# Stage B of a graph layer: rows that chunks 2 and 3 share with the next round's chunks 0 and 1 are summed there, and a load stands ahead of a wait

## What is computed

```python
h = relu(layernorm(x))
x = x + mean_over_edges(h[src] -> dst) @ W_l.T + h @ W_r.T      # layer 0, stage A
h = relu(layernorm(x))                                          # layer 1, stage B
agg = segment_sum(edge_attr, src, num_segments=N)
h = concatenate([h, agg], axis=1)
h = bn(silu(h @ W1 + b1))                                       # stage C, statistics over all nodes
h = bn(silu(h @ W2 + b2))                                       # stage F
x = x + h @ W3 + b3                                             # stage G
```

## Time and profile before

| | |
|---|---|
| median of three runs | 1505.77 us |
| the profiled execution, its own time | 1503.21 us |
| its span | 1501.3 us |
| POOL busy | 828.5 us, 55% |
| DVE busy | 1099.7 us, 73% |
| PE busy | 1021.5 us, 68% |
| ACT busy | 862.9 us, 57% |
| granted TensorE clock, mean | 0.918 |
| line 848, B's scatter | 196 instructions, 314.7 us busy, 168.5 us idle ahead of them |

### The profile page before, as it was taken

The page is one execution under the profiler, slowest core; times in us unless marked ns, Lnnn a source line. Parts: engine busy times, 40 slices in busy tenths (PEclk is TensorE's granted clock), DMA queues, the critical chain, the costliest instruction groups (busy, mean ns, idle before and its releaser), DMA issues.

```text
span 1501.3 us, 22959 instructions
## 1 busy us (share of the span) xinstructions
PE 1021.5 (68%) x5247; PEld 726.3 (48%) x5247; DVE 1099.7 (73%) x4644; ACT 862.9 (57%) x1686; POOL 828.5 (55%) x601
## 2 busy tenths in 40 slices
PE   0237767677666667658777777776657877997866
PEld 0125555555544455435444444444435765446755
DVE  1438888888867766669788878776764877778978
ACT  0226777777755555537666666656564545665533
POOL 6778887888888888766666667655551000000000
PEclk9959999999999988969999999889997998999989
DMA  9988898877766666677777777899987996207999
GB/s 277 386 275 220 204 228 211 187 166 169 170 146 142 135 144 143 140 159 199 196 195 197 193 195 198 234 264 273 268 247 250 348 333 234 97 28 260 407 403 373
DMA packets 225365, 333.72 MB, mean 222 GB/s; under 512 B 35778, under 2 KB 87242, under 8 KB 225300
## 3 DMA queue, kind: packets, MB, share of 16 engines
q1 hardware_dynamic: 157516, 285.22, 56.1%
q0 software_dynamic: 62720, 38.57, 20.4%
q10 hardware_dynamic: 5064, 9.29, 1.7%
HBM read 179.20 MB, written 153.80 MB: 222 GB/s over the span
## 4 chain that ended last, share of the span: by engine, by line
POOL 41%; DMA 26%; issue 16%; PE 10%; DVE 5%; SPq 1%; ACT 1%; POOLq 0%; DVEq 0%; ACTq 0%
POOL acc L833 20%; POOL acc L848 11%; DMA acc<-zT,target_b 8%; DMA acc<-tabs,target_b 8%; POOL xin L811 7%; PE ps L1538 6%; POOL zT L819 4%; DMA zT<-x_dram 3%; DMA xin<-acc 2%; PE ps L1548 1%; DMA acc<-zT,tabs 1%; DVE zT L1383 1%; DVE zT L1387 1%; PE ps L1514 1%; PE ps L1517 1%
## 5 line engine op out<-in xcount | busy, mean ns | idle before, releaser
L1430 PE MATMUL ps<-zT 128*128 128x512 f32 (+5 forms) x784 | 278.0, 505 | 196.4 <-ACT zT L951 135.4
L833 POOL DMA_INDIRECT acc<-zT,tabs x196 | 314.8, 1606 | 71.5 <-issue 64.6
L1430 PEld LDWEIGHTS ps<-zT 128*128 128x128 f32 (+1 forms) x784 | 162.6, 217 | 338.8 <-issue 208.8
L848 POOL DMA_INDIRECT acc<-zT,target_b x100 | 161.0, 1610 | 87.1 <-DMA acc<-zT,target_b 32.5
L1153 DVE SCALAR_TENSOR_TENSOR zT<-zT 128x128 f32<-128x128 f32 (+3 forms) x392 | 192.9, 548 | 12.7 <-DMA zT<-row_dram 6.4
L1221 DVE BATCH_NORM_STATS2 zT<-zT 128x6 f32<-128x128 f32 (+1 forms) x384 | 78.9, 278 | 165.3 <-DMA zT<-in_x_dram 165.3
L848 POOL DMA_INDIRECT acc<-tabs,target_b x96 | 153.7, 1601 | 81.4 <-issue 32.0
L811 POOL DMA_INDIRECT xin<-in_x_dram,tabs x140 | 141.9, 1014 | 47.3 <-issue 42.4
L1422 PE MATMUL ps<-ident,zT 128*128 128x128 f32 (+1 forms) x784 | 111.5, 288 | 65.4 <-ACT zT L904 65.4
L1422 PEld LDWEIGHTS ps<-ident,zT 128*128 128x128 f32 (+1 forms) x784 | 92.2, 149 | 78.4 <-ACT zT L904 75.7
L1548 PE MATMUL ps<-w,hT 128*128 128x128 f32 (+1 forms) x784 | 101.5, 285 | 38.2 <-DVE zT L1387 28.7
(11 more groups left out here) (159 smaller groups left out, 2017.0 us busy)
## 6 DMA issues: line engine op xcount, KB each, us to landing
acc<-bst SPq DMA_DIRECT2D x12, 2112.0 KB, 21.5
acc<-bst SPq DMA_DIRECT2D x48, 528.0 KB
zT<-row_dram SPq DMA_DIRECT2D x98, 256.0 KB, 5.7
zT<-in_x_dram SPq DMA_DIRECT2D x48, 512.0 KB, 6.7
zT<-acc SPq DMA_DIRECT2D x48, 512.0 KB, 4.3
zT<-x_dram SPq DMA_DIRECT2D x42, 512.0 KB, 8.5
out_dram<-zT SPq DMA_DIRECT2D x42, 512.0 KB, 7.7
zT<-in_edge_attr_dram SPq DMA_DIRECT2D x48, 256.0 KB, 6.4
```

The lines of the kernel that those rows point to most:

```text
L833: pool.indirect_dma_start(acc1, bass.IndirectOffsetOnAxis(ap=target_a[:, k, j:j + 1], axis=0), v[:, j, :], None, compute_op=ALU.add).then_ ...
L848: pool.indirect_dma_start(acc2, bass.IndirectOffsetOnAxis(ap=target_b[:, k, j:j + 1], axis=0), vrow_b[k % RING][:, j, :], None, compute_op ...
L1430: ins = nc.tensor.matmul(psA[:, 0:j + 1, 0:p], t[0:p, j, :], same[0:p, par, at:at + j + 1, 0:p], start=(j == ROWS - 1), stop=(j == 0))
```

## The change

In B, the rows of **chunks 2 and 3** that the next round names again are moved there. Chunk 3's are added into chunk 0 or chunk 1 of the next round, chunk 2's into its chunk 0. DVE gets one more comparison for each round (line 1188 of the new code, two chunks of names against chunk 3's), and `more`, `alone` and the corrected `count` are two columns wide. PE gets three products where it had one. POOL's chunk 0 then awaits chunks 0 and 1 of the round before, chunk 1 awaits chunk 2 (`s_mid2`), chunk 2 awaits chunk 3. The new matrices lie in `bst`, which also holds the zeros that clear `acc2`; so the first pair that is compared is rounds 1 and 2, round 1's chunk 0 awaits all of round 0, and DVE awaits the clearing ahead of B's rounds. SP's load of `acc1`'s rows stands ahead of the wait for chunk 3's landing, no longer behind it. Two pairs of semaphores of C and G become one pair, with the counts added.

```diff
@@ step_b, SP
                 i, par, tail, spill, slot = now
-                sp.wait_ge(*this(s_end2, par, i, 16))
                 if ahead:
                     load_b_nodes(*ahead)
+                sp.wait_ge(*this(s_end2, par, i, 16))
                 sp.wait_ge(*this(B["added"], par, i))
@@ scatter_b, POOL
                 if k:
-                    pool.wait_ge(*last(s_sc2, par, i, 48))
+                    pool.wait_ge(*last(s_sc2, par, i, 32))
+                if k == 1:
+                    pool.wait_ge(*last(s_mid2, par, i, 16))
+                    pool.wait_ge(*last(s_end2, par, i, 16))
                 for j in range(ROWS):
-                    if k and j == 1:
+                    if k > 1 and j == 1:
+                        pool.wait_ge(*last(s_mid2, par, i, 16))
+                    if k > 1 and j == 2:
                         pool.wait_ge(*last(s_end2, par, i, 16))
...
-                        .then_inc((s_end2 if j == ROWS - 1 else s_sc2)[par], 16)
+                        .then_inc((s_sc2, s_sc2, s_mid2, s_end2)[j][par], 16)
@@ compare_carry, DVE
+                nc.vector.scalar_tensor_tensor(
+                    carried_3[par][:, :, 0:p], irow[:, par, 0:2, 0:p], cols[:, before, 0, ROWS - 1:ROWS],
+                    alone[:, before, 1:2].unsqueeze(2).broadcast_to([P, 2, p]), ALU.is_equal, ALU.mult,
+                    accum_out=more[:, par, 1:2])
                 link_(nc.vector.scalar_tensor_tensor(
-                    carried[par][:, 0:p], irow[:, par, 0, 0:p], cols[:, before, 0, ROWS - 1:ROWS],
-                    alone[:, before:before + 1].broadcast_to([P, p]), ALU.is_equal, ALU.mult,
-                    accum_out=more[:, par:par + 1]))
+                    carried_2[par][:, 0:p], irow[:, par, 0, 0:p], cols[:, before, 0, ROWS - 2:ROWS - 1],
+                    alone[:, before, 0:1].broadcast_to([P, p]), ALU.is_equal, ALU.mult,
+                    accum_out=more[:, par, 0:1]))
@@ ahead of B's rounds, DVE
+            dve.wait_ge(s_zero2, 16 * RF)
@@ edge_product, PE
-                    given = carry is not None and j == 0
...
+                    taken_over = [] if carry is None or j > 1 else [(carried_3[par][:, j, :], ROWS - 1)]
+                    if taken_over and j == 0:
+                        taken_over.append((carried_2[par], ROWS - 2))
```

More of the change, by code:

```diff
@@ L203, in gnn_layers @@
         iota_c = part([P, COLS // 2]).bitcast(fp16)
-        carried = [iota_c[:, :].bitcast(fp32)[:, 0:P], tabs[:, 2 * GROUP:2 * GROUP + P]]
         cols = part([P, 2, 4, ROWS])
         count = sb("count", [P, 2, ROWS])
-        more = sb("more", [P, 2])
-        alone = sb("alone", [P, 2])
+        more = sb("more", [P, 2, 2])
+        alone = sb("alone", [P, 2, 2])
         shift = sb("shift", [P, 2, ROWS])
@@ L220, in gnn_layers @@
         bst = sb("bst", [P, 2 * (RF + 1), 6])
+        carried_2 = [iota_c[:, :].bitcast(fp32)[:, 0:P], tabs[:, 2 * GROUP:2 * GROUP + P]]
+        carried_3 = [bst[:, :, :].rearrange("p a s -> p (a s)")[:, k * 2 * P:(k + 1) * 2 * P]
+                     .rearrange("p (c q) -> p c q", q=P) for k in range(2)]
         zeros = bst[:, :, :].rearrange("p a s -> p (a s)")[:, 0:ZCOLS]
@@ L260, in gnn_layers @@
         x1_stored = [sem(f"b_x1_stored_{k}") for k in range(RING)]
-        C = phase("c", "transposed added silu stats stored")
+        C = phase("c", "transposed added silu stats")
+        C["stored"] = pair("c_z_stored_then_g_early_out_stored")
         F = phase("f", "product silu stats stored")
-        G = phase("g", "scaled product done stored early_stored")
+        G = phase("g", "scaled product done stored")
         acc2_loaded = [pair(f"acc2_loaded_{k}") for k in range(2)]
@@ L270, in gnn_layers @@
         s_sc2 = pair("acc2_scattered")
+        s_mid2 = pair("acc2_third_chunk_scattered")
         s_end2 = pair("acc2_last_chunk_scattered")
@@ L620, in _ @@
             sweep(sp, step_b, (KEPT,), wide=True, margin=2)
-            sp.wait_ge(*this(s_sc2, 0, IT, 48))
-            sp.wait_ge(*this(s_sc2, 1, IT - 1, 48))
+            sp.wait_ge(*this(s_sc2, 0, IT, 32))
+            sp.wait_ge(*this(s_sc2, 1, IT - 1, 32))
+            sp.wait_ge(*this(s_mid2, 0, IT, 16))
+            sp.wait_ge(*this(s_mid2, 1, IT - 1, 16))
             sp.wait_ge(*this(s_end2, 0, IT, 16))
@@ L765, in _ @@
             for par in range(2):
[L766 removed]
+                sp.wait_ge(C["stored"][par], 16 * (IT - KEPT_LATER + (0 if par else 2) + EARLY_G))
             for i, par, tail in late_rounds():
@@ L1477, in multiply_edges_b @@
                 pe.wait_ge(*last(B["v_copied"], par, i))
-                first = type(i) is int and i == 0 and par == 0
+                first = type(i) is int and i == 0
                 edge_product(w1b, par, tail, None if first else vrow_b[(slot - 1) % RING]).then_inc(B["v_ready"][par], 1)
```

32 lines of the change are left out of this document (14 added, 18 removed).

## The result

The changed kernel takes **1524.21 us**, the median of four runs (1519.53 to 1526.51). The kernel before took 1506.87 beside it (four runs, 1505.55 to 1508.4). The ratio is 1.012, with a 95% interval of 1.0099 to 1.014. So it is 17 us slower, where 31 us less had been forecast.

A forecast was written before the change was run, and what follows sets the result against it. POOL's scatters and their landings were taken to bound B, DVE next. Terms +0.4 (rounds 0 to 5), -5.5 (6 to 29), -3.5 (30, 31), -20.8 (32 to 47), -2 (end) made -31.4: 1474 us, range 1460 to 1497.

The forecast's parts named there:

- The added comparison, and DVE's rounds: DVE in B: the 256-column comparison adds 0.40 us a round; peeled rounds 8.35 us, looped rounds 9.14 us.
- PE at nothing: PE in B: two more products of 128 columns, 0.4 us, keep it level with DVE and cost nothing.
- POOL's loop, "L + 1.85": POOL's scatters in B: a round falls by 1.85 us, to 7.55 in the first half and 8.95 in the second.
- L: Time from an awaited scatter's start to the dependent start in B: 5.7 us in the first half, 7.1 in the second.
- The load ahead of the wait costs nothing else: SP in B: the load goes out when its buffer is free; only longer scatter landings remain as an open cost.
- the rise of L: Scatter landings in B: the moved loads lengthen L by between nothing and 1.4 us.
- the 1.6 us of room: First half of B: L may grow by 1.6 us before POOL's loop passes DVE's 9.14 us.
- The gain that I did see: DVE in B: loads of `acc1` and `y` no longer end its idle time, 0.56 to 3.52 us where they did.
- DMA's floor of 9.25 to 9.5 us: Spilled rounds of B: transfers bound a round at 9.25 us; 9.5 taken, from 10.80, -20.8 us over 16 rounds.
- The end of B, -2: Round 48's last scatter, awaited by C's loads, starts sooner: 2 us less, ends 0 and 4.3.
- (c): Rival, B's scatters: the load's packets lengthen landings by over 1.85 us; at +2.5 us, 26 us slower, 1532 us; 5%.
- the sum would have been 1497: B's second half: slower memory access adds up to 1.8 us per landing and returns that step, -9 us in all.

The follow-up runs named there:

- e3: The changed kernel with SP's wait for chunk 3's landing removed from B's rounds, accumulator load before x1's store: 1482.44 us, ratio 0.981.
- e13: The changed kernel without SP's wait for chunk 3's landing, x1's store before the accumulator load: 1486.91 us, ratio 0.9802.
- e1: The changed kernel with SP's accumulator load put back behind the wait for chunk 3, so the moved rows alone: 1500.99 us, ratio 0.9968.
- e9: The changed kernel with a 256 KB copy of the features added to each burst: 1521.64 us, ratio to the kernel before 1.0083.
- e4: The kernel before without SP's wait for chunk 3's landing, accumulator load before x1's store: 1552.83 us, ratio 1.0273.
- e18: The kernel before without SP's wait for chunk 3's landing, x1's store before the accumulator load: 1523.87 us, ratio 1.0055.
- e6: The changed kernel with the accumulator load behind the wait for chunk 3 and x1's store written ahead of it: 1504.19 us, ratio 0.9988.
- e14: The changed kernel with all four transfers behind the wait, in the order x1 store, names, accumulator load, features: 1533.33 us, ratio 1.0095.
- e16: The changed kernel with all four transfers behind the wait, in the order x1 store, features, accumulator load, names: 1499.03 us, ratio 0.9959.
- e11: The changed kernel with 240 KB of features left out of each burst in the looped rounds: 1507.88 us, ratio to the kernel before 0.9995.

## Why the prediction was wrong

**The added comparison, and DVE's rounds: right.** The 256-column comparison steps by 661.12 - 660.71 = 0.41 us (timeline, round 0), 0.40 forecast:

```profile
660.71 0.48 DVE L1188 SCALAR_TENSOR_TENSOR bst<-zT,alone 128x256 f32<-128x256 f32 x1
661.12 0.08 DVE L1188 DVE_READ_ACCUMULATOR bst<-zT,alone 128x1 f32 x1
```

Where DVE isn't held (e3, e13) a looped round takes 9.05 and 9.04 us, 9.14 forecast. The changed kernel never gets there in the first half.

**PE at nothing: nothing speaks against it.** In e3 the same products run within DVE's 9.05 us.

**POOL's loop, "L + 1.85": its form was right, L was wrong.** This is the first step that failed. I took L, 5.7 us, from the chunk that was awaited before (chunk 2, sent 3.7 us behind chunk 0, with which the burst starts) and gave it to chunk 1, which is sent 1.85 behind it. By the chain, chunk 1 needs 777.48 - 769.94 = 7.54 us to the next chunk 0, of which 777.48 - 776.68 = 0.80 is POOL's wake. 1.84 + 7.54 = 9.38 us, and the gain of 1.85 is gone. Of the 1.8 us that L is short, about 0.6 stood in the trace of the kernel before: chunk 1 took 5.5 us to land there at the median of the odd rounds, 6.3 with the wake. The other 1.2 came with the change: to 6.3 us of landing at the median of e1's chain, with the moved rows, and to 6.75 in the changed kernel's, with the load behind the names. Nor was the median of rows 9 a figure for L: it mixes all four chunks. The burst on SP's queue, in the timeline of SP that I hadn't put beside POOL's, would have warned too: its last transfer was issued at 779.33 and features took 5.9 us to land (row in the last section), so all was through at 785.2, with chunk 2's 785.44.

In the first half L had room to spare, and with the old order of the burst the forecast for it held (e1, 9.04 us). In the spilled rounds it had none: 7.1 us had been put there, and e1's chain has 7.9 us of landing alone.

**The second loop, not seen.** The new wait of chunk 2 for chunk 3 makes a loop of its own, chunk 3, its landing, the next chunk 2, 1.85 us, chunk 3. I had counted it among the waits and given it no time. In the changed kernel's spilled rounds it binds most often: 1035.82 - 1025.19 = 10.63 us, then 1047.54 - 1035.82 = 11.72, with landings of 8.52 and 9.61. Its chain goes through chunk 3 in 10 of these rounds; that of e1, with the old order, goes through chunk 1 in 15 of 16.

**"The load ahead of the wait costs nothing else": wrong**, by 23 us. Two claims failed in it. The load isn't free of the wait, since the one before it on SP's queue holds it; it goes in the burst, last. And the rise of L, 0 to 1.4 us, was right in size (the period grew by 0.54 us from e1 to the changed kernel in both halves: 9.04 to 9.58 and 10.49 to 11.03), but the 1.6 us of room that I gave the first half weren't there, because L already stood near 7.1 with the moved rows alone (6.3 us of landing and 0.8 of wake). The gain that I did see, loads that no longer end DVE's idle time, came true for `acc1` only. DVE's waits in 706 to 1134 us (us in total, times, longest) have none for it at line 1305, and still one for `y` in each spilled round:

```profile
DVE res L1305 <- DMA res<-y_dram: 21.2, 8, 5.0
DVE xin L1305 <- DMA xin<-y_dram: 13.5, 8, 2.1
```

**DMA's floor of 9.25 to 9.5 us: not reached by the change.** e13 doesn't speak against it. Its spilled rounds have a POOL period of 9.39, and the share is 1.06:

```profile
954.00:1092.00 138.00, 110.53 (x536) 76.38 (x535) 126.01 (x673) 101.16 (x207) 90.44 (x57) 0.96 1.06 309
```

**The end of B, -2: wrong**, +1.1, since POOL still lags there.

**The rivals.** (c) comes nearest, at 5%. Its point of decision, L = 7.5 us in the first half, is where the changed kernel stands (7.54). I had set it beside landings of 5.5 and 7.2, which leave out POOL's wake and mix all four chunks. Its mechanism is right in part: packets of the burst lengthen the landings, but in the first half it is the names' place in it, not the load's meeting the scatters at another time, and the moved rows lengthen the landings too.

On the page of the Trainium skill cited in the prediction (DMA: Bandwidth & Descriptors, Latency and other measured facts): by its figure for memory access (0.2 to 2 us) the sum would have been 1497. Chunk 1's landing went from 5.5 to 6.7 us at the median of the odd rounds, 1.2 us more and so within that figure's 1.8, but with the mean traffic at 192 GB/s against 196. What the mean doesn't tell is what was under way just then. Another rule of the Trainium skill (DMA: Bandwidth & Descriptors, Queues, rings and completion order) bears on that: a transfer's semaphore increment is a strongly ordered write, and lands only after every earlier write of that DMA engine, across its queues. That would make a small scatter finish with a burst issued just ahead of it. The trace agrees in part. In the changed kernel the load issued at 779.60 took 6.2 us and so landed at 785.8, and chunk 1, whose issue runs from 779.33 to 780.96, landed at 786.1, 8.65 us behind its chunk 0. But chunk 0, issued with the burst's first transfer, landed at 784.3, ahead of the load, and before the change chunk 1 landed 7.65 us behind chunk 0. No run here tests the rule itself, and e9 doesn't follow from it alone.

## What to carry to other kernels

- When a wait is moved from a later transfer to an earlier one, read when the earlier one lands, not how long the later one takes. Next to a burst of another queue the earlier one may take longer: here chunks 0, 1 and 2, sent 1.85 to 2.2 us apart, landed 6.0, 7.65 and 8.2 us behind chunk 0's start.
- A landing that releases both a scatter and another queue's burst locks the two together. Take the lock away and measure, rather than move one transfer across the wait. It gained 2% with the moved rows (e3, e13) and lost without them (e4, e18).
- A transfer written ahead of a wait still stands behind the wait of the step before. Look in the queue's timeline where it really goes (the load here, the store in e6).
- Each new wait may close a loop of its own; write down every loop with its own landing.

## What the runs showed of the hardware

- **The order of transfers in a burst counts**, with the same bytes. From the burst's first issue to chunk 1's landing, which lets the next chunk 0 go, it took 785.28 - 777.22 = 8.06 us with the load first (e1), 802.59 - 793.93 = 8.66 with the names before the load (e14). The features in the same place cost nothing (e16). The load of the names fills 128 partitions from one row of 2 KB. In the changed kernel the load from `acc1` lands in 6.2 us at the median where it had 4.3, and x1's store in 3.1 where it had 5.2 (720 to 900 us). The first lines are of the kernel before, the next two of the changed one (KB each, median us to landing):

```profile
zT<-acc SPq DMA_DIRECT2D x20, 512.0 KB, 4.3
x_dram<-res SPq DMA_DIRECT2D x10, 512.0 KB, 5.2
...
zT<-in_edge_attr_dram SPq DMA_DIRECT2D x19, 256.0 KB, 5.9
```

```profile
zT<-acc SPq DMA_DIRECT2D x19, 512.0 KB, 6.2
x_dram<-res SPq DMA_DIRECT2D x10, 512.0 KB, 3.1
```

  Why the names' place matters inside the DMA engines isn't shown: no run changed how the names are laid out.
- **256 KB more in each burst cost nothing** (e9, 218 GB/s in 720 to 900 us against 192), although 240 KB less relieved the first half (e11). The cost was in the pattern and not in the sum.
- **A median of landings can mislead.** In the kernel before the profile has a landing for chunks 0, 1 and 2 in the odd rounds and for chunk 3 in the even ones, so the 5.5 us of rows 9 is a mixture. Chunk by chunk the medians of rounds 6 to 29 are 6.8, 5.5, 4.2 and 3.45 us. In the changed kernel all four chunks have one in every round; the odd rounds give 6.7, 6.7, 5.15 and 3.65.
